# A two-channel order on TensorE and an earlier hand-over of the operands, in a fused pair-block and feed-forward kernel

## The reference

```
ab1, ab2, ab3 = gate_proj(zn, ...) * zm      # from x, three projections
pp, lp, ip    = gate_proj(...)               # from protein_pair, l_pair, inter_pair
block = einsum('bikc,bkjc->bijc', pp, ab1) + einsum('bikc,bjkc->bijc', ab2, lp) + ab3 * ip
out   = sigmoid(zn @ Wend + bend) * (ln(block) @ Wsum + bsum) * zm
x = x + out
# then: routing over 8 experts from token means, a feed-forward of each token, layer norm, residual
```

## Time and profile before

| | us |
|---|---|
| time, median of 3 runs | 1477.86 |
| lowest, highest | 1474.34, 1480.62 |
| the profiled execution's own time | 1476.01 |
| its span, first to last instruction | 1474.3 |
| PE busy (share) | 1361.6 (92%) |
| DVE busy | 1225.5 (83%) |
| POOL busy | 1007.1 (68%) |
| ACT busy | 983.9 (67%) |
| mean granted TensorE clock | 0.974 |

### The profile page before, as it was taken

One profiled execution on the slowest core, in us unless ns is written; L12 is line 12 of the kernel. 1 busy time (PEld: TensorE's weight loads), 2 busy tenths in 40 slices (PEclk: granted clock), 3 DMA queues, 4 the chain that ended last, 5 costly groups with the idle time before them and its releaser, 6 DMA issues. The chain is left out here.

```text
span 1474.3 us, 32179 instructions
## 1 busy us (share of the span) xinstructions
PE 1361.6 (92%) x9869; PEld 1134.6 (77%) x9869; DVE 1225.5 (83%) x4155; ACT 983.9 (67%) x2293; POOL 1007.1 (68%) x1555
## 2 busy tenths in 40 slices
PE   5999999999999986899789999499999999999993
PEld 2877778877778865788666666389999999999983
DVE  6998999998999863677699999567888888888996
ACT  3888888888888864344367777246677676776763
POOL 3999999999999984445378888324555555555663
PEclk9999999999999998999999999799999999999997
DMA  9999999999999978989689996211222322232222
GB/s 212 209 261 247 261 237 256 244 258 254 255 244 249 244 191 258 282 273 289 181 254 299 297 299 198 104 30 44 86 72 72 87 72 87 72 85 74 73 57 72
DMA packets 358375, 270.63 MB, mean 184 GB/s; under 512 B 60710, under 2 KB 333054, under 8 KB 358206
## 3 DMA queue, kind: packets, MB, share of 16 engines
q1 hardware_dynamic: 356924, 268.16, 69.4%
q10 hardware_dynamic: 1010, 0.20, 0.1%
q0 software_dynamic: 272, 0.21, 0.1%
HBM read 174.16 MB, written 94.37 MB: 182 GB/s over the span
## 5 line engine op out<-in xcount | busy, mean ns | idle before, releaser
L1467 ACT ACTIVATE hT<-psH_d,b 128x512 f32<-128x512 f32 x288 | 198.0, 688 | 162.6 <-PE psH_d L1502 162.4
L1489 PE MATMUL psY_d<-w,hT 128*128 128x128 f32 x2304 | 268.9, 275 | 0.0
L1489 PEld LDWEIGHTS psY_d<-w,hT 128*128 128x128 f32 x2304 | 263.0, 192 | 0.1
L642 PE MATMUL psZ_a<-w_all,xT_a 128*128 128x128 f32 x1728 | 232.0, 278 | 4.9 <-DVE low_pp L717 4.9
L642 PE MATMUL psZ_a<-w_all,xT_block 128*128 128x384 f32 x576 | 214.6, 496 | 8.4 <-DVE low_ab L711 5.5
L642 PEld LDWEIGHTS psZ_a<-w_all,xT_a 128*128 128x128 f32 x1728 | 211.9, 193 | 7.5 <-issue 5.1
L566 ACT ACTIVATE sig_a<-psZ_a 128x256 f32<-128x256 f32 (+1 forms) x360 | 153.4, 426 | 88.1 <-PE psZ_a L642 51.2
L578 POOL TENSOR_SCALAR shared<-shared,coefs_early 128x128 f32<-128x128 f32 x468 | 203.2, 449 | 0.0
L629 PE MATMUL psT_a<-ident,shared 128*128 128x128 f32 x1152 | 187.0, 275 | 3.4 <-issue 2.0
L629 PEld LDWEIGHTS psT_a<-ident,shared 128*128 128x128 f32 x1152 | 142.1, 142 | 54.3 <-issue 27.7
L1526 POOL TENSOR_TENSOR u_d<-u_d,gamma 128x512 f32<-128x512 f32 x72 | 96.0, 1333 | 124.9 <-ACT u_d L1453 109.6
(11 more groups left out here) (218 smaller groups left out, 2940.7 us busy)
## 6 DMA issues: line engine op xcount, KB each, us to landing
shared<-in_x_dram SPq DMA_DIRECT2D x48, 512.0 KB, 5.7
scratch_xT<-xT_block SPq DMA_DIRECT2D x36, 512.0 KB, 5.3
shared<-scratch_xT SPq DMA_DIRECT2D x36, 512.0 KB, 5.0
scratch_x<-x_c SPq DMA_DIRECT2D x36, 512.0 KB, 4.2
shared<-scratch_x SPq DMA_DIRECT2D x36, 512.0 KB, 3.6
shared<-in_x_dram SPq DMA_DIRECT2D x48, 256.0 KB, 5.2
shared<-L_conv_protein_pair_dram SPq DMA_DIRECT2D x24, 512.0 KB, 7.6
shared<-in_L_conv_l_pair_dram SPq DMA_DIRECT2D x24, 512.0 KB, 8.9
```

The lines of the kernel that those rows point to most:

```text
L642: ins = nc.tensor.matmul(out, turned_x(G, i, t0, size)[:, j * P:j * P + P], rhs[i], start=True, stop=True)
L1467: nc.scalar.activation(hT[:, S % 2, f, :], psH[:, f, :], ACT.Gelu, bias=s["b1"][:, f:f + 1]).then_inc(gelued, 1)
L1489: ins = nc.tensor.matmul(psY[:, G % 2, i * CH:i * CH + CH], hT[:, G % 2, f, i * P:i * P + P], s["w2"][:, f, :], start=(f == 0), stop=(f == ...
```

## The change

Two edits. In `triangle_phase`, PE's program is written by pairs: the low matmuls of both channels, then the high matmuls of both, then the turn of the next pair. Conditions for the matmuls are the same semaphores with the same values. In `project_phase`, the last block has an SP program of its own. The xT stores and the pp and lp stores of block 10 follow the thirds of the x pass as in the other blocks, and stand ahead of the first operand loads. The last 16 rows' columns are no longer loaded all together at the end: those of ab1, ab2, pp and mov_high follow the ab and pp stores, then sta_high's first columns once three groups of ip have been turned, and only lp_low's and sta_high's last columns wait for the lp store. The final waits for the xT stores are now behind all loads.

```diff
+STA_GROUPS = -(-OPERAND // (PASSES[3][2] * CH))
...
-            def body(n, last):
+            def body(n):
...
+            def last_body(n):
+
+                early, late = (0, N - BLOCK_A), (N - BLOCK_A, N)
+                of_ab, of_pp, of_lp = (("ab1_high", "ab1_low", "ab2_low"), ("pp_low", "mov_high"), ("lp_low",))
+                for k in range(len(CHUNKS)):
+                    sp.wait_ge(turned, NG_A * n + PASS_START[0] + CHUNKS[k][1] // PASSES[0][2])
+                    store_xT(n, k)
+                    if k < 2:
+                        store_out(n - 1, k + 1)
+                sp.wait_ge(stored[0], 48 * n)
+                load_operands(OPERANDS[0:2], *early)
+                store_out(n, 0)
+                for i in range(1, 3):
+                    sp.wait_ge(turned, NG_A * n + PASS_END[i])
+                    sp.wait_ge(stored[i], 48 * n)
+                    load_operands(OPERANDS[2 * i:2 * i + 2], *early)
+                    store_out(n, i)
+                sp.wait_ge(stored[0], 48 * NBLK)
+                load_operands(of_ab, *late)
+                sp.wait_ge(stored[1], 48 * NBLK)
+                load_operands(of_pp, *late)
+                sp.wait_ge(turned, NG_A * n + PASS_START[3] + STA_GROUPS)
+                load_operands(OPERANDS[6:], *early)
+                sp.wait_ge(stored[2], 48 * NBLK)
+                load_operands(of_lp + OPERANDS[6:], *late)
+
+            for n in range(NBLK - 1):
+                body(n)
+            last_body(NBLK - 1)
             for k in range(len(CHUNKS)):
                 sp.wait_ge(stored_xT[k], 16 * NBLK)
-            for i in range(3):
-                sp.wait_ge(stored[i], 48 * NBLK)
-            load_operands(OPERANDS, N - BLOCK_A, N)
...
             turn(0)
-            for C in range(HID):
-                Q, e = divmod(C, 2)
-                if e == 0:
-                    pe.wait_ge(copied, Q + 1)
...
-                ins.then_inc(summed, 1)
-                if e == 0 and Q + 1 < PAIRS_B:
+            for Q in range(PAIRS_B):
+                pe.wait_ge(copied, Q + 1)
+                pe.wait_ge(packed_act, Q + 1)
+                pe.wait_ge(packed_pool, Q + 1)
+                pe.wait_ge(packed_dve, Q + 1)
+                for e in range(2):
+                    C = 2 * Q + e
+                    need(pe, taken, 2 * (C - 3))
+                    for k, (sta, mov) in enumerate(sides(Q, e)):
+                        nc.tensor.matmul(psO[:, C % 4, 0:N], sta[:, 0:P], mov, start=(k == 0), stop=(k == 2))
+                for e in range(2):
+                    C = 2 * Q + e
+                    for k, (sta, mov) in enumerate(sides(Q, e)):
+                        for h in range(2):
+                            ins = nc.tensor.matmul(psO[64 * h:64 * h + 64, C % 4, N:N + N // 2], sta[:, P:N], high_half(mov, h),
+                                                   start=(k == 0), stop=(k == 2))
+                    ins.then_inc(summed, 1)
+                if Q + 1 < PAIRS_B:
                     turn(Q + 1)
```

More of the change, by code:

```diff
@@ L488, in _ @@
                     load_third(i, k, 0)
-            def body(n, last):
+            def body(n):
                 for i in range(len(PASSES)):
[L492 to L505, removed]
-                        if i == 0:
[L507 to L512, removed]
+                    for k in range(len(CHUNKS)):
+                        sp.wait_ge(turned, NG_A * n + PASS_START[i] + CHUNKS[k][1] // PASSES[i][2])
+                        load_third(i, k, n + 1)
+                        if i == 0:
+                            store_xT(n, k)
+                            if n > 0 and k < 2:
+                                store_out(n - 1, k + 1)
@@ L513, in body @@
                     if i == 0:
                         store_out(n, 0)
-            for n in range(NBLK):
-                body(n, n == NBLK - 1)
+            def last_body(n):
+                early, late = (0, N - BLOCK_A), (N - BLOCK_A, N)
+                of_ab, of_pp, of_lp = (("ab1_high", "ab1_low", "ab2_low"), ("pp_low", "mov_high"), ("lp_low",))
+                for k in range(len(CHUNKS)):
+                    sp.wait_ge(turned, NG_A * n + PASS_START[0] + CHUNKS[k][1] // PASSES[0][2])
+                    store_xT(n, k)
+                    if k < 2:
+                        store_out(n - 1, k + 1)
+                sp.wait_ge(stored[0], 48 * n)
[14 more added lines that the diff above has]
+                load_operands(of_lp + OPERANDS[6:], *late)
@@ L813, in _, with high_half @@
                     load_tiles(sp, mix_buffers(s)[0][:, p], d["x"], p, s["loaded_x"][p][k], ch)
+        def high_half(mov, h):
+            return mov.rearrange("p (n u) -> p n u", u=LOW)[:, :, HIGH * h:HIGH * h + HIGH]
         @block.tensor
@@ L832, in turn, with sides @@
                 ins.then_inc(turned, 1)
+            def sides(Q, e):
+                return [(sta[:, Q % 2, e, :], mov[:, Q % 2, e, :]) for sta, mov in ((ab1T, pp_now), (lp_now, ab2_now), (sta_now, mov_now))]
             turn(0)
-            for C in range(HID):
-                Q, e = divmod(C, 2)
-                if e == 0:
-                    pe.wait_ge(copied, Q + 1)
[L839 to L851, removed]
-                ins.then_inc(summed, 1)
-                if e == 0 and Q + 1 < PAIRS_B:
```

## The result

The changed kernel takes 1488.34 us (median of 4 runs, 1486.67 to 1490.46) against 1477.86 us: a ratio of 1.0075, 95% interval 1.0052 to 1.0098. It is slower by some 11 us. The profiled execution takes 1486.67 us, its span 1484.9 us against 1474.3.

A forecast was written before the change was run, and what follows sets the result against it. PE was taken to pace the triangle stage at 4.31 us a pair, with two waits at the seam before it. +24.9 - 11.5 = +13.4 us on 1476.0 gives 1489.4, plus 1.9 to the median 1491.3, said as 1490; range 1477 to 1503.

The forecast's parts named there:

- the two parts: Triangle stage with the new order on PE, +24.9 us; projection's end and hole behind it, 11.5 us gained.
- The uncovered copies: Triangle stage: PE waits for ACT's copies of the turned pair, a new stall of 1.38 us, pairs of 5.35 us.
- My bounds for the stall: Triangle stage: PE's new stall in each pair lies between 1.15 and 1.6 us.
- The sign that I named: Triangle stage: PE idle before each pair's first low matmul, released by ACT, 1.2 to 1.5 us, 31 times.
- The saved switches: Triangle stage: two switches less in a pair, PE's own work 3.97 us against 4.31, 0.34 us saved.
- Rival (a): Triangle stage: switches cost more than the gaps show, and their loss pays for the stall; 1479 us, chance 0.12.
- rival (d): Triangle stage: the order on PE yields no saving, a switch being paid at the weight load anyway; 1501 us, chance 0.04.
- The operand waits: Triangle stage: the 7.0 us of waits for operands and half clock after one go; none left, 4 us as bound.
- The stores first: Projection's last block: DVE's wait for the pp store and what follows go, 7.9 us; projection ends at 556.0.
- The last columns: Hole ahead of the triangle: seven of nine loads moved forward, 3.5 us less issue; with stores first, start at 563.5.
- rival (b): Triangle stage: the clock falls as PE rests 1.38 us in each pair; 1506 to 1540 us, chance 0.12.

The follow-up runs named there:

- e3: Changed kernel with the next pair's turn moved between the low and the high matmuls: 1463.96 us, ratio 0.9921 against the kernel before.
- e10: Changed kernel with operand loads of only the first 48 of 192 columns from the third group on: 1489.42 us, ratio 1.0086.
- e2: Changed kernel with the old SP program of the projection, so only the new order on PE: 1497.48 us, ratio 1.0147.
- e11: Old order on PE, last block's stores first, but all nine last-column loads together behind all stores: 1468.18 us, ratio 0.9937.
- e7: e3 with seven last-column loads (ab1, ab2, pp, mov_high) issued from ACT's queue instead of SP's: 1466.05 us, ratio 0.9927.
- e1: Changed kernel with PE's old program of the triangle, so only the new last block on SP: 1465.5 us, ratio 0.993.
- e6: e3 with operand loads of only the first 48 of 192 columns from the third group on: 1452.22 us, ratio 0.9829.

## Why the prediction was right, and where its steps were off

The forecast was 1490 and +13.4 us, the result 1488.3 and +10.5; the direction and the mechanism hold, and the two parts came out at +19.2 and -9.5 us where +24.9 and -11.5 were forecast.

**The uncovered copies: right, the size of one step wrong.** I forecast pairs of 5.35 us, measured are 5.16. Two terms of the sum were off. The first is the hand-over from ACT to PE, for which I took 0.22 us from the end of a copy to the weight load, and 0.11 to the matmul. In the changed kernel the copy ends at 646.54 + 0.47 = 647.01 and the matmul starts at 647.07: 0.06 us. The row I had read was no wait for a copy. Between the two rows that I quoted stands another of the same trace, PE's own transposes of the next group:

```profile
553.24 0.47 PEld L629 LDWEIGHTS psT_a<-ident,shared 128*128 128x128 f32 x4
```

PE's weight loads are busy with it until 553.71, and the load at 553.68 comes right behind it; the copy had been done since 553.46. A true hand-over stands some microseconds further on, at a place where the weight loads are marked idle for the copy (which ends at 559.92 + 0.57 = 560.49):

```profile
560.54 0.97 PEld L642 LDWEIGHTS psZ_a<-w_all,xT_a 128*128 128x128 f32 x8 [0.18 <-ACT xT_a L550]
560.54 1.16 PE L642 MATMUL psZ_a<-w_all,xT_a 128*128 128x128 f32 x8
```

That is 0.05 us. The second term runs the other way: a low part that follows a pause takes 644.06 - 641.91 = 2.15 us for the two channels, not 2.06, since its first weight load is uncovered as after a switch. So from the turn's start to the next matmul it is 1.87 and not 2.15 (-0.28), the low parts take +0.09: 5.35 - 0.19 = 5.16. Over 32 pairs this is 6 us, and accounts for 167.6 against the 173.3 us of the forecast. My bounds for the stall did not hold: the new stall is 1.87 - 0.77 = 1.10 us against 1.15 to 1.6, and no run shows the 0.2 us of the upper bound for a PE that sleeps. The sign that I named, PE idle for 1.2 to 1.5 us 31 times, came as 31 times 0.94.

**The saved switches: right.** PE's own work in a pair was forecast at 3.97 us; a pair of e3 in which nothing pauses has 3.96. Its two high parts take 648.42 - 647.28 = 1.14 us, 0.64 and 0.50 as I estimated, but my reason (half the columns) was short: twelve instructions of 96 columns are as many columns as six of 192. They start 0.17 us apart for an operand, where the low ones take 0.33, so the two halves' matmuls run side by side. Rival (a), that a drain costs more than the gaps show, is thereby refuted, and rival (d), that nothing is saved, falls too. The Trainium skill, TensorEngine Tiling (Array Packing), section Key Properties, has it that a change of tiling mode drains the engine; this case puts a price to it, 0.35 us for two switches fewer in a pair, and no more.

**The operand waits: right that they go.** None is left in the changed kernel, and e10 shows that bytes have no part in its time. That they went by the new order and not by the seam is e2's result.

**The stores first: right.** Forecast 7.9 us and an end of the projection at 556.0; the end is at 555.58, and at 556.83 in e11, where the stores alone are moved. The wait of the earlier trace rows is gone in both.

**The last columns: the term was too large.** I forecast a start at 563.5 and measured 565.44, a hole of 9.9 us instead of 7.5. The step that was off is the sum of bytes over a rate of 289 GB/s: the DMA engines moved 171 GB/s in the hole, at a share of 0.69, so bytes did not bind to its end. Two things that I had counted on did not come. The issues in front of the lp store's landing were not free: ten loads in one row, for which I had allowed 0.5 us each, took from 553.93 to 562.41. And sta_high's first part was not issued inside the inter pass, but behind seven of them at 560.70, 5 us after the projection's end. e7, in which both are changed, has the hole at 6.87. What holds the rest I did not separate.

**The clock: rival (b) did not occur.** With a pause of 0.94 us on PE in each pair, the granted clock was 1.00 from 584 to 734. By the Trainium skill, TensorE: Matmul & The Clock Gate, section on psum-queue depth-cycling, frequent small pauses of PE would have had it swing; this trace does not agree. Where the clock did fall was behind some of the longer waits for operands: in e7 it is 0.50 from 677 to 681, behind a wait of 3.41 us.

The errors of the two parts have opposite signs (-5.7 in the stage, +2.0 at the seam), and the stages behind it added 0.9; so the sum, -2.8, looks better than its terms. That it came so near is in part luck.

## What to carry to other kernels

Before work of an engine is reordered, ask what each piece of it was covering: here two switches saved were worth 0.35 us a pair, and the odd channel's matmuls that had hidden two copies were worth 1.1. Put the turn between the two kinds of matmuls, and both are served: the switches stay saved, and the high matmuls cover the copies. And before the next 11 us are taken from an engine, look at the share of the DMA engines: at 0.97 the gain stopped at the transfers here, as e3 against e1 and e6 shows. Of these kernels e3 and e1 are the ones to use, 0.8% and 0.7% faster than the kernel before.

## What the runs showed of the hardware that I had not expected

- The hand-over from the end of an ACT copy to a waiting PE matmul takes 0.05 to 0.06 us at full clock (at 560.54 in the kernel before, at 647.07 in the changed one), a quarter of the 0.22 that I had read.
- ACT copies in a row start 0.37 us apart though each is recorded with 0.48 us; a copy more cost the waiting PE 0.37 to 0.38 (5.16 to 5.54 us a pair).
- Four loads of 32 to 64 KB took 5.12 us to issue while the operand loads and stores issued ahead of them were under way (changed kernel, 553.93), where nine such loads took 4.9 us once these had landed (e11, 560.43). Small DMAs moved forward cost SP more here than they did behind.
- PE's pauses of 0.94 us in every 5.16 us left its clock at 2.4 GHz (granted clock 1.00 from 584 to 734). Some waits of 1.85 to 3.4 us were followed by the 1.2 GHz level (0.50 from 616 to 618 in the kernel before, behind 1.85 us), others were not (1.00 from 584 to 604 there, with the 2.02 us in it).
